# Expert loops of a mixture-of-experts layer, taken in steps of two pairs of tiles instead of one, with weights addressed in bytes

## The chip, the cores and the metric

The kernel runs on one NeuronCore of a Trainium2 chip. The metric is the device time of one launch in microseconds (us). PE is TensorE, DVE VectorE, ACT ScalarE, POOL GpSimd and SP SyncE, which computes nothing here and issues transfers. PEld is TensorE's loading of weights, which overlaps its products.

## The reference

The input is 128 sequences of 125 time steps with 64 channels. Three layers follow: a strided depthwise convolution with a norm over the whole sequence, a selective scan, and a mixture of experts. Only the last matters here; its core is, for 8064 tokens (128 x 63) of 64 channels:

```python
logits = xf @ Wr + br                                  # 64 experts
topk_logits, topk_idx = jax.lax.top_k(logits, 2)
gates = jax.nn.softmax(topk_logits, axis=1)
combine = zeros((T, E)).at[arange(T)[:, None], topk_idx].add(gates)
for e in range(E):
    h = relu(xf @ W1[e] + b1[e])                       # 64 -> 128
    y = h @ W2[e] + b2[e]                              # 128 -> 64
    out = out + combine[:, e:e + 1] * y
```

All of it is in float32.

## The kernel before

The kernel doesn't compute every expert for every token. It runs the experts' layers once for the tokens' first choice and once for their second (two halves). For each half it sorts the tokens by expert: VectorE works out a row number for every token, and GpSimd scatters the token rows to DRAM (`sorted_rows`), 63 indirect transfers of 128 rows each (line 438). Each expert's rows are padded to whole tiles of 128 rows, so a half has 126 tiles at most; two tiles are a pair, and a half has 63 pairs (`PAIRS`), 126 in all. The number of each tile's expert is worked out on the chip too and stands in `te`.

The expert stage goes over the 126 pairs. For each of them

- SyncE loads the packed weights of the two tiles' experts (first layer, second layer and bias beside each other, 193 floats per row, 128 rows) with two transfers (`load_weights`, line 328) into one of `WRING` = 7 slots, at an address read from a register. Before slot n % 7 is loaded again, SyncE waits until the outputs of pair n - 7 are copied out (`s_yb`). The expert numbers come into registers 32 at a time, once every 16 pairs (line 274). Token rows come for four pairs at once (`load_rows`, line 337), in a ring of four.
- TensorE transposes the pair's 128 x 128 block of token rows (`rows_T`, line 593), does the first-layer products of its two tiles, each on 64 rows of the array (`hidden`, line 600), and the output products (`outputs`, line 611), 192 columns wide, of which 64 are wanted.
- ScalarE copies the transposed block (`xT_copy`, line 812) and does bias and relu of the first tile (`relu_A`, line 819); VectorE does bias and relu of the second (`relu_B`, line 1162) and copies the outputs out (`y_copy`, line 1172). A float32 product shows as two matrix instructions in the trace, so a pair has one transpose, four first-layer and four output instructions.
- ScalarE's queue stores the outputs to DRAM (`store`, line 827, `expert_out`), from a ring of four (`YRING`).

The order on each engine is written out by hand: transposes run two pairs ahead of the outputs, first-layer products one pair ahead.

GpSimd's own order is: scatter of the first half, scatter of the second, gather of the first half's outputs (line 446) when its stores have landed, gather of the second half's. Each gather is again 63 indirect transfers. SyncE loads the first rows of the second half only when the second scatter has landed (`s_disp`). When gathered rows arrive, VectorE applies the gates and adds them up, and the result leaves.

Of the kernel before, what the change touches and what calls it, by code (L numbers as in the profile page):

```python
# [7 lines left out]
U32 = mybir.dt.uint32  # L8
ALU = mybir.AluOpType
# [4 lines left out]
P = 128  # L14
T_IN = 125
C = 64
# [31 lines left out]
WRING = 7  # L48
YRING = 4
WROW = HID + C + 1  # L50
OUT = 3 * C
CQ = -(-L // 8)
IDS = 32

# [21 lines left out]
def build(nc, x, w, b, gamma, beta, alpha, A_log, D_param, scale, W_dt, b_dt, W_B, b_B, W_C, b_C,  # L76
# [5 lines left out]
    with ExitStack() as ctx:  # L82
# [75 lines left out]
        xT_e = x_w1[:, o:o + 2 * P].rearrange("p (k n) -> p k n", k=2)  # L158
        o += 2 * P
        hT_e = x_w1[:, o:o + 4 * P].rearrange("p (k t n) -> p k t n", k=2, n=P)  # L160
        o += 4 * P
        y_e = x_w1[:, o:o + YRING * 2 * C].rearrange("p (k t d) -> p k t d", k=YRING, d=C)
# [109 lines left out]
        def experts(engine, g):  # L272

            return nc.values_load_multi_w_load_instructions(te[0:1, bass.ds(g, IDS)], engines=[engine],
                                                            min_val=0, max_val=E - 1, skip_runtime_bounds_check_because=
                                                            "te is a count of experts, clamped to E - 1")[1]
# [4 lines left out]
        def _(sp):  # L281
# [39 lines left out]

            def load_weights(h, q, es):

                n = h * PAIRS + q
                if n >= WRING:
                    sp.wait_ge(s_yb, n - WRING + 1)
                for t in range(2):
                    sp.dma_start(w_in[:, n % WRING, t, :], packed[bass.ds(es[t], 1), :, :].rearrange("a p n -> (a p) n")  # L328
                                 ).then_inc(s_win[n % WRING], 16)

            def load_rows(h, u):

                n = h * UNITS + u
                if n >= RING:
                    g, v = (n - RING) // UNITS, (n - RING) % UNITS
                    sp.wait_ge(s_rT, g * PAIRS + min(UNIT * (v + 1), PAIRS))
# [29 lines left out]
        def _(pool):  # L366
# [75 lines left out]
            for k, y in enumerate((y1, y2)):  # L442
                for j in range(YRING):
                    pool.wait_ge(s_st[j], 16 * (((k + 1) * PAIRS + YRING - 1 - j) // YRING))
# [7 lines left out]
        def _(pe):  # L452
# [135 lines left out]
            def rows_T(n):  # L588

                u = unit_of(n)  # L590
                if n % PAIRS % UNIT == 0:
                    pe.wait_ge(s_rows[u % RING], 16 * (u // RING + 1))
                pe.transpose(ps[:, n % 2, 0:P], rows_in[:, u % RING, n % PAIRS % UNIT, :], ident[:, :]).then_inc(s_rT, 1)  # L593

            def hidden(n):

                pe.wait_ge(s_win[n % WRING], 32 * (n // WRING + 1))
                pe.wait_ge(s_rTc, n + 1)
                for t in range(2):
                    last = pe.matmul(ps[:, 2 + 2 * (n % 2) + t, 0:P], w_in[t * C:(t + 1) * C, n % WRING, t, 0:HID],  # L600
                                     xT_e[t * C:(t + 1) * C, n % 2, :], start=True, stop=True)
                last.then_inc(s_hid, 1)

            def outputs(n):

# [4 lines left out]
                for t in range(2):  # L610
                    last = pe.matmul(ps[:, 6 + n % 2, t * OUT:(t + 1) * OUT], hT_e[:, n % 2, t, :],  # L611
                                     w_in[:, n % WRING, t, 0:OUT], start=True, stop=True)
# [14 lines left out]
            pe.wait_ge(s_yb, 2 * PAIRS)  # L627
# [24 lines left out]
        def _(act):  # L652
# [156 lines left out]
            def xT_copy(n):  # L809

                act.wait_ge(s_rT, n + 1)
                act.activation(xT_e[:, n % 2, :], ps[:, n % 2, 0:P], ACT.Copy).then_inc(s_rTc, 1)  # L812

            def relu_A(n):
# [425 lines left out]
```

## Time and profile before

| | |
|---|---|
| median of 3 runs | 884.67 us (881.72 to 885.47) |
| the profiled execution | 888.75 us |
| its span, first to last instruction | 886.8 us |
| PE, DVE, ACT, POOL busy | 501.2, 645.4, 339.2, 551.6 us |
| DMA traffic | 71.63 MB |
| mean granted clock of TensorE | 0.741 of full speed |

The profile comes from one execution, and its durations add up to its own time. Busy times are averages over stages with different limits: the convolution and the norms up to about 139 us, the scan up to about 446 us, routing and the first scatter up to about 612 us, the expert stage from 615 to about 797 us, the second gather and the sum up to the end. The expert stage is the one in which the change lies, and it is read from its own stretch.

### The profile page before, as it was taken

To read this page: it belongs to the slowest core of one execution; us is meant where nothing else is said; L and a number is where in the kernel's file an instruction comes from. 1 tells how busy PE (TensorE), PEld (TensorE's weight loads), DVE (VectorE), ACT (ScalarE), POOL (GpSimd) and SP (SyncE) were. 2 spreads that over 40 slices of the span, in tenths; PEclk is the share of its full clock that TensorE was granted. 3 is DMA by queue.
4 is the path that set the end of the run, shared out by engine and by line. 5 is a ranking of instruction groups with operands and counts; after the bars stand their busy time and mean duration, and the time that the engine had idled before them with its cause. 6 is when DMAs were issued, how large, how long until landed. Compare 5 with 4: busy or idle time off the path is not lost.

```text
span 886.8 us, 8725 instructions
## 1 busy us (share of the span) xinstructions
PE 501.2 (57%) x2132; PEld 320.0 (36%) x2132; DVE 645.4 (73%) x1160; ACT 339.2 (38%) x597; POOL 551.6 (62%) x398
## 2 busy tenths in 40 slices
PE   4916903365666665575556920002999999980340
PEld 3815801121211121121116910001777777760240
DVE  1379548999999989999974999991444444459951
ACT  2311384555555455454527710000444444430110
POOL 1002204699999999999940007777777167757774
PEclk9965655677787787878785555555999999995565
DMA  6999900000000000000000000302899899961131
GB/s 229 366 136 108 30 0 0 0 0 0 1 0 0 0 0 0 0 0 0 0 0 1 1 0 27 89 25 62 229 262 265 230 256 263 269 192 26 25 99 37
DMA packets 100734, 71.63 MB, mean 81 GB/s; under 512 B 29330, under 2 KB 87314, under 8 KB 100690
## 3 DMA queue, kind: packets, MB, share of 16 engines
q1 hardware_dynamic: 73154, 54.39, 28.0%
q0 software_dynamic: 8064, 8.27, 3.5%
q10 hardware_dynamic: 19472, 8.47, 3.3%
q8 instruction: 16, 0.26, 0.1%
q14 instruction: 28, 0.23, 0.1%
HBM read 48.12 MB, written 29.29 MB: 87 GB/s over the span
## 4 chain that ended last, share of the span: by engine, by line
POOL 35%; PE 22%; DVE 15%; issue 15%; SPq 4%; DMA 4%; ACT 3%; POOLq 1%; DVEq 0%; ACTq 0%
POOL hh_ring L419 13%; PE ps L611 8%; POOL w_ring L404 8%; POOL sorted_rows L438 7%; POOL xt L446 7%; PE ps L600 4%; DMA x_w<-packed 3%; PE ps L470 3%; SPq L328 2%; PE ps L538 2%; DVE mi L1072 1%; PE ps L521 1%; PE ps L593 1%; DVE hh_ring L1004 1%; DVE w_ring L1060 1%
## 5 line engine op out<-in xcount | busy, mean ns | idle before, releaser
L538 PE MATMUL ps<-hh_ring,ident 128*128 128x512 f32 x272 | 181.7, 807 | 153.1 <-POOL hh_ring L419 116.4
L438 POOL DMA_INDIRECT sorted_rows<-xp,slot_i x126 | 122.1, 969 | 115.0 <-DVE slot_i L1098 76.9
L404 POOL TENSOR_TENSOR w_ring<-xt,bc 128x1024 f32<-128x1024 f32 x64 | 153.8, 2405 | 37.3 <-DVE xt L973 37.3
L446 POOL DMA_INDIRECT xt<-expert_out,slot_i x126 | 120.7, 958 | 65.6 <-issue 37.8
L419 POOL TENSOR_TENSOR hh_ring<-hh_ring,bc 128x1024 f32<-128x1024 f32 x63 | 148.4, 2356 | 17.9 <-DVE hh_ring L1004 14.6
L538 PEld LDWEIGHTS ps<-hh_ring,ident 128*128 128x128 f32 x272 | 58.2, 234 | 275.8 <-POOL hh_ring L419 184.7
L1004 DVE TENSOR_TENSOR_SCAN hh_ring<-ps,w_ring 128x1024 f32<-128x1024 f32 x64 | 145.9, 2280 | 0.1
L611 PE MATMUL ps<-x_w 128*128 128x192 f32 x504 | 117.0, 355 | 0.0
L744 ACT ACTIVATE ps<-dt_t,a_exp 128x1024 f32<-128x1024 f32 x64 | 71.5, 1118 | 79.9 <-DVE w_ring L982 79.9
L748 ACT ACTIVATE ps<-dt_t,a_exp 128x1024 f32<-128x1024 f32 x64 | 71.5, 1118 | 65.1 <-DVE hh_ring L1004 65.1
L1172 DVE COPY x_w<-ps 128x128 f32<-128x128 f32 x126 | 36.8, 292 | 72.0 <-PE ps L611 69.0
L812 ACT ACTIVATE x_w<-ps 128x128 f32<-128x128 f32 x126 | 34.9, 278 | 135.1 <-PE ps L593 134.4
L611 PEld LDWEIGHTS ps<-x_w 128*128 128x128 f32 x504 | 79.7, 191 | 15.2 <-issue 0.4
L982 DVE TENSOR_TENSOR w_ring<-ps,w_ring 128x1024 f32<-128x1024 f32 x64 | 78.3, 1224 | 8.4 <-POOL w_ring L404 4.2
L998 DVE SCALAR_TENSOR_TENSOR w_ring<-ps,w_ring 128x1024 f32<-128x1024 f32 x64 | 76.8, 1200 | 0.0
L1162 DVE TENSOR_SCALAR x_w<-ps,x_w 128x128 f32<-128x128 f32 x126 | 44.3, 351 | 42.8 <-PE ps L600 40.4
L390 POOL TENSOR_TENSOR us_lg<-xp,vecs 128x1344 f32<-128x1344 f32 x3 | 9.2, 3069 | 88.5 <-DVE xp L926 88.5
L600 PE MATMUL ps<-x_w 64*128 64x128 f32 x504 | 62.9, 327 | 2.3 <-DMA x_w<-packed 1.8
L819 ACT ACTIVATE x_w<-ps,x_w 128x128 f32<-128x128 f32 x126 | 46.3, 368 | 24.1 <-PE ps L600 21.9
L600 PEld LDWEIGHTS ps<-x_w 64*128 64x128 f32 x504 | 38.7, 188 | 31.3 <-issue 25.3
L593 PE MATMUL ps<-ident,x_w 128*128 128x128 f32 x126 | 34.8, 278 | 16.7 <-DMA x_w<-sorted_rows 16.7
L584 PE MATMUL ps<-ident,tile_e 128*1 128x128 f32 x2 | 0.7, 373 | 55.6 <-DVE tile_e L1138 55.6
(174 smaller groups left out, 707.9 us busy)
## 6 DMA issues: line engine op xcount, KB each, us to landing
x_w<-packed SPq DMA_DIRECT2D x252, 96.5 KB
sorted_rows<-pad_rows SPq DMA_DIRECT2D x2, 4096.0 KB, 18.0
x_w<-sorted_rows SPq DMA_DIRECT2D x32, 256.0 KB
expert_out<-x_w ACTq DMA_DIRECT2D x126, 64.0 KB
packed<-in_L_ffn_W SPq DMA_DIRECT2D x3, 2048.0 KB, 36.2
x_w<-in_x SPq DMA_DIRECT2D x7, 448.0 KB, 10.1
sorted_rows<-xp,slot_i POOLq DMA_INDIRECT x126, 2.1
xt<-expert_out,slot_i POOLq DMA_INDIRECT x126, 2.4
```

The lines of the kernel that those rows point to most:

```text
L404: pool.tensor_tensor(w_ring[:, k % 4, :].rearrange("p (d s) -> p d s", s=S), up3[:, bass.ds(c * DC, DC), :], bc[:, k:k + 1, :].broadcast_t ...
L419: pool.tensor_tensor(hc_buf(k), h_buf(k), bc[:, N + k:N + k + 1, :].broadcast_to([P, DC, S]), ALU.mult).then_inc(s_hcp, 1)
L438: pool.indirect_dma_start(out=sorted_rows[k], out_offset=bass.IndirectOffsetOnAxis(ap=slot_i[:, k, l:l + 1], axis=0), in_=xp1[:, l, 0:C], ...
L446: pool.indirect_dma_start(out=y[:, l, :], out_offset=None, in_=expert_out[k], in_offset=bass.IndirectOffsetOnAxis(ap=slot_i[:, k, l:l + 1] ...
L538: ins = pe.matmul(ps[:, i, :], ident[:, :], hh_ring[:, buf, i * BANK:(i + 1) * BANK], start=(k < 0), stop=(k == N - 1), skip_group_check=True)
L600: last = pe.matmul(ps[:, 2 + 2 * (n % 2) + t, 0:P], w_in[t * C:(t + 1) * C, n % WRING, t, 0:HID], xT_e[t * C:(t + 1) * C, n % 2, :], start ...
L611: last = pe.matmul(ps[:, 6 + n % 2, t * OUT:(t + 1) * OUT], hT_e[:, n % 2, t, :], w_in[:, n % WRING, t, 0:OUT], start=True, stop=True)
L744: act.activation(banks(6, 2), d, ACT.Tanh, scale=a_exp[:, 2, k:k + 1]).then_inc(s_th, 1)
L748: act.activation(banks(2 + 2 * (k % 2), 2), d, ACT.Exp, scale=a_exp[:, 1, k:k + 1]).then_inc(s_dA, 1)
L982: dve.tensor_tensor(wv, banks(6, 2), wv, ALU.mult).then_inc(s_g, 1)
L998: dve.scalar_tensor_tensor(out=wv, in0=dA, scalar=1.0, in1=wv, op0=ALU.add, op1=ALU.mult).then_inc(s_b, 1)
L1004: dve.tensor_tensor_scan(hh_ring[:, k % 2, :], dA, wv, 0.0, ALU.mult, ALU.add).then_inc(s_h, 1)
```

## The change

Every loop of the expert stage goes in steps of two pairs (the 63rd pair of each half is a step of its own, so a half has 32 steps). In a step TensorE does two transposes into one PSUM bank, then eight first-layer instructions, then eight output instructions, which write both output banks (6 and 7) where one bank was used before. The semaphores count steps. ScalarE copies both transposed blocks with one instruction and does two bias-and-relu instructions; VectorE does two, and copies the outputs of both pairs with one; one store takes both. The weights' ring has eight slots instead of seven and is given back in steps: the weights of step i wait for the outputs of step i - 4. Slots of transposed rows, hidden rows and outputs are twice as large, as many as before.

`te` holds the expert's number times the bytes of an expert's block (98,816), multiplied on VectorE for all tiles at once. The weight transfers read the packed weights as bytes at that offset, where they read floats of block number e before.

```diff
-WRING = 7
+WRING = 8
 YRING = 4
+STEPS = -(-PAIRS // 2)
+BLOCK = 4 * P * WROW
+def pairs_of(i):
+    h, d = divmod(i, STEPS)
+    return range(h * PAIRS + 2 * d, h * PAIRS + min(2 * d + 2, PAIRS))
+def step_of(n):
+    return n // PAIRS * STEPS + n % PAIRS // 2
...
+            blocks = packed.rearrange("e p n -> (e p n)").bitcast(U8)
             def load_weights(h, q, es):
                 n = h * PAIRS + q
                 if n >= WRING:
-                    sp.wait_ge(s_yb, n - WRING + 1)
+                    sp.wait_ge(s_yb, step_of(n - WRING) + 1)
                 for t in range(2):
-                    sp.dma_start(w_in[:, n % WRING, t, :], packed[bass.ds(es[t], 1), :, :].rearrange("a p n -> (a p) n")
+                    sp.dma_start(w_in[:, n % WRING, t, :].bitcast(U8),
+                                 blocks[bass.ds(es[t], BLOCK)].rearrange("(p n) -> p n", p=P)
                                  ).then_inc(s_win[n % WRING], 16)
...
-            def hidden(n):
-                pe.wait_ge(s_win[n % WRING], 32 * (n // WRING + 1))
-                pe.wait_ge(s_rTc, n + 1)
-                for t in range(2):
-                    last = pe.matmul(ps[:, 2 + 2 * (n % 2) + t, 0:P], w_in[t * C:(t + 1) * C, n % WRING, t, 0:HID],
-                                     xT_e[t * C:(t + 1) * C, n % 2, :], start=True, stop=True)
+            def hidden(i):
+                for n in pairs_of(i):
+                    pe.wait_ge(s_win[n % WRING], 32 * (n // WRING + 1))
+                pe.wait_ge(s_rTc, i + 1)
+                for j, n in enumerate(pairs_of(i)):
+                    for t in range(2):
+                        last = pe.matmul(ps[:, 2 + 2 * (i % 2) + t, j * P:(j + 1) * P],
+                                         w_in[t * C:(t + 1) * C, n % WRING, t, 0:HID],
+                                         xT_e[t * C:(t + 1) * C, i % 2, j, :], start=True, stop=True)
                 last.then_inc(s_hid, 1)
-            def outputs(n):
-                pe.wait_ge(s_reluA, n + 1)
-                pe.wait_ge(s_reluB, n + 1)
-                if n >= 2:
-                    pe.wait_ge(s_yb, n - 1)
+            def outputs(i):
+                pe.wait_ge(s_reluA, i + 1)
+                pe.wait_ge(s_reluB, i + 1)
+                if i >= 1:
+                    pe.wait_ge(s_yb, i)
...
-            for n in range(2 * PAIRS):
-                if n + 2 < 2 * PAIRS:
-                    rows_T(n + 2)
-                if n + 1 < 2 * PAIRS:
-                    hidden(n + 1)
-                outputs(n)
+            for i in range(2 * STEPS):
+                if i + 2 < 2 * STEPS:
+                    rows_T(i + 2)
+                if i + 1 < 2 * STEPS:
+                    hidden(i + 1)
+                outputs(i)
...
-                dve.tensor_scalar(te[:, k * P:(k + 1) * P], ps[0:1, 2, 0:P], float(E - 1), None, ALU.min
+                dve.tensor_scalar(te[:, k * P:(k + 1) * P], ps[0:1, 2, 0:P], float(E - 1), float(BLOCK), ALU.min, ALU.mult
                                   ).then_inc(s_tei, 1)
```

On TensorE, in the middle of the expert stage, this stood before, for two pairs (`x_w1` holds the weights and the token rows, `ps` is PSUM; a matrix product here is one row):

```order
L593 MATMUL ps<-ident,x_w1 128x128
L600 MATMUL ps<-x_w1 128x128 [waits s_rTc,s_win4]
L600 MATMUL ps<-x_w1 128x128
L611 MATMUL ps<-x_w1 128x192 [waits s_yb,s_reluB,s_reluA]
L611 MATMUL ps<-x_w1 128x192
L593 MATMUL ps<-ident,x_w1 128x128
L600 MATMUL ps<-x_w1 128x128 [waits s_rTc,s_win5]
L600 MATMUL ps<-x_w1 128x128
L611 MATMUL ps<-x_w1 128x192 [waits s_yb,s_reluB,s_reluA]
```

And this stands on TensorE now, for one step:

```order
L610 MATMUL ps<-ident,x_w1 128x128 x2
L621 MATMUL ps<-x_w1 128x128 [waits s_rTc,s_win5,s_win4]
L621 MATMUL ps<-x_w1 128x128 x3
L634 MATMUL ps<-x_w1 128x192 [waits s_yb,s_reluB,s_reluA]
L634 MATMUL ps<-x_w1 128x192 x3
```

Each kind of product now stands in runs twice as long, and the first-layer run waits for the weights of both pairs at its start.

On SyncE, where the first loads wait for a slot, two pairs' weights stood before as (the ISA row multiplies the register):

```order
L328 ISA [waits s_yb]
L328 DMA x_w1<-packed 128x193
L328 ISA
L328 DMA x_w1<-packed 128x193
L328 ISA [waits s_yb]
L328 DMA x_w1<-packed 128x193
L328 ISA
L328 DMA x_w1<-packed 128x193
L337 DMA x_w1<-sorted_rows0 128x512
```

Now they stand on SyncE as:

```order
L343 DMA x_w1<-packed 128x772 [waits s_yb]
L343 DMA x_w1<-packed 128x772
L343 DMA x_w1<-packed 128x772 [waits s_yb]
L343 DMA x_w1<-packed 128x772
L353 DMA x_w1<-sorted_rows0 128x512 [waits s_rT]
```

The register instruction is gone; both waits of a step are for the same count, that of step i - 4, where each pair waited for its own before.

## Rows read from the trace of the kernel before

**Rows 1.** The page's head: span, and busy time of each engine.

```profile
span 886.8 us, 8725 instructions
PE 501.2 (57%) x2132; PEld 320.0 (36%) x2132; DVE 645.4 (73%) x1160; ACT 339.2 (38%) x597; POOL 551.6 (62%) x398
```

**Rows 2.** Windows: stretch, length, busy time (instructions) by engine, clock, DMA share, GB/s.

```profile
core 0: us, PE busy (x) PEld busy (x) DVE busy (x) ACT busy (x) POOL busy (x), PEclk, DMA share, GB/s
640.00:660.00 20.00, 19.71 (x131) 14.81 (x130) 9.16 (x29) 9.19 (x29) 15.13 (x17) 1.00 0.94 264
700.00:720.00 20.00, 19.47 (x127) 14.57 (x127) 9.02 (x29) 9.04 (x29) 6.05 (x7) 1.00 0.87 239
```

**Rows 3.** Timeline of one pair: start, length, engine, line, tiles, count, idle before.

```profile
652.64 0.27 PE L593 MATMUL ps<-ident,x_w 128*128 128x128 f32 x1
652.84 0.49 PE L600 MATMUL ps<-x_w 64*128 64x128 f32 x4
653.26 0.92 PE L611 MATMUL ps<-x_w 128*128 128x192 f32 x4
...
654.02 0.27 PE L593 MATMUL ps<-ident,x_w 128*128 128x128 f32 x1
...
654.29 0.29 DVE L1172 COPY x_w<-ps 128x128 f32<-128x128 f32 x1 [0.56 <-PE ps L611]
```

**Rows 4.** Timelines of TensorE over short stretches, same columns.

```profile
622.48 0.76 PE L611 MATMUL ps<-x_w 128*128 128x192 f32 x3
...
652.84 0.38 PE L600 MATMUL ps<-x_w 64*128 64x128 f32 x2
...
653.06 0.28 PE L600 MATMUL ps<-x_w 64*128 64x128 f32 x2
...
793.42 1.57 PE L611 MATMUL ps<-x_w 128*128 128x192 f32 x8
```

**Rows 5.** Waits in the expert stage: us in total, times, longest.

```profile
PEld ps L600 <- DMA x_w<-packed: 6.0, 15, 1.0
```

**Rows 6.** SyncE: instructions by line (ns minimum/median/maximum), a timeline row, its waits.

```profile
L328 SPq FUSED_REGOPS  x252: 37/37/51, 555.2 to 787.1; - x126
L328 SPq MOVE x_w<-packed x252: 29/29/38, 555.3 to 787.2; - x126
L328 SPq DMA_DIRECT2D x_w<-packed x252: 332/333/1693, 555.4 to 787.2; - x126
...
L337 SPq DMA_DIRECT2D x_w<-sorted_rows x32: 332/436/484, 612.1 to 780.6; - x32
...
L274 SPq TENSOR_LOAD <-te x8: 1916/2028/2227, 553.1 to 767.3; - x8
...
641.74 3.95 SPq L328 DMA_DIRECT2D x_w<-packed  x8
...
SPq L328 <- DVE x_w L1172: 11.1, 11, 6.4
```

**Rows 7.** The chain that ended last: start, length, what; transfers from issue to use.

```profile
612.07 2.77 DMA x_w<-sorted_rows
...
644.31 5.73 DMA x_w<-packed
...
727.27 3.23 DMA x_w<-packed
...
777.01 3.63 DMA x_w<-packed
```

**Rows 8.** Ends of scatters, turn of the halves, starts of gathers (chain and timelines).

```profile
609.91 2.14 DMA sorted_rows<-xp,slot_i
...
690.02 0.97 POOL L438 DMA_INDIRECT sorted_rows<-xp,slot_i  x1 [0.30 <-issue]
...
707.45 0.27 PE L593 MATMUL ps<-ident,x_w 128*128 128x128 f32 x1
708.75 0.33 ACTq L827 DMA_DIRECT2D expert_out<-x_w  x1
...
712.11 0.98 POOL L446 DMA_INDIRECT xt<-expert_out,slot_i  x1 [21.12 <-DMA expert_out<-x_w]
...
797.68 0.95 POOL L446 DMA_INDIRECT xt<-expert_out,slot_i  x1 [6.70 <-DMA expert_out<-x_w]
```

More of the change, by code:

```diff
@@ L8 @@
 U32 = mybir.dt.uint32
+U8 = mybir.dt.uint8
 ALU = mybir.AluOpType
@@ L274, in experts @@
             return nc.values_load_multi_w_load_instructions(te[0:1, bass.ds(g, IDS)], engines=[engine],
-                                                            min_val=0, max_val=E - 1, skip_runtime_bounds_check_because=
-                                                            "te is a count of experts, clamped to E - 1")[1]
+                                                            min_val=0, max_val=(E - 1) * BLOCK,
+                                                            skip_runtime_bounds_check_because="te is a count of experts, "
+                                                            "clamped to E - 1, times the bytes of a block")[1]
         block = ctx.enter_context(nc.Block())
@@ L443, in _ @@
                 for j in range(YRING):
-                    pool.wait_ge(s_st[j], 16 * (((k + 1) * PAIRS + YRING - 1 - j) // YRING))
+                    pool.wait_ge(s_st[j], 16 * (((k + 1) * STEPS + YRING - 1 - j) // YRING))
                 for l in range(L):
@@ L604, in outputs, with rows_T @@
-            def outputs(n):
-                pe.wait_ge(s_reluA, n + 1)
-                pe.wait_ge(s_reluB, n + 1)
-                if n >= 2:
-                    pe.wait_ge(s_yb, n - 1)
-                for t in range(2):
-                    last = pe.matmul(ps[:, 6 + n % 2, t * OUT:(t + 1) * OUT], hT_e[:, n % 2, t, :],
-                                     w_in[:, n % WRING, t, 0:OUT], start=True, stop=True)
+            def rows_T(i):
+                for j, n in enumerate(pairs_of(i)):
+                    u = unit_of(n)
+                    if n % PAIRS % UNIT == 0:
+                        pe.wait_ge(s_rows[u % RING], 16 * (u // RING + 1))
+                    last = pe.transpose(ps[:, i % 2, j * P:(j + 1) * P], rows_in[:, u % RING, n % PAIRS % UNIT, :],
+                                        ident[:, :])
+                last.then_inc(s_rT, 1)
@@ L613, in outputs @@
+            def outputs(i):
[3 more added lines that the diff above has]
+                    pe.wait_ge(s_yb, i)
+                for j, n in enumerate(pairs_of(i)):
+                    for t in range(2):
+                        last = pe.matmul(ps[:, 6 + j, t * OUT:(t + 1) * OUT], hT_e[:, i % 2, t, j, :],
+                                         w_in[:, n % WRING, t, 0:OUT], start=True, stop=True)
                 last.then_inc(s_yps, 1)
@@ L832, in _ @@
             relu_A(0)
-            for n in range(2 * PAIRS):
-                if n + 2 < 2 * PAIRS:
-                    xT_copy(n + 2)
-                if n + 1 < 2 * PAIRS:
-                    relu_A(n + 1)
-                if n > 0:
-                    store(n - 1)
-            store(2 * PAIRS - 1)
+            for i in range(2 * STEPS):
+                if i + 2 < 2 * STEPS:
+                    xT_copy(i + 2)
+                if i + 1 < 2 * STEPS:
+                    relu_A(i + 1)
+                if i > 0:
+                    store(i - 1)
+            store(2 * STEPS - 1)
             for q in range(CQ):
```

84 lines of the change are left out of this document (43 added, 41 removed).

## The prediction

> **What bounds the kernel now.** I read the page's head first: no engine is busy for more than 73% of the 886.8 us [rows 1], so stages have to be read one by one. The change touches the expert stage, from about 615 to 797 us. The windows of that stage show TensorE busy all the time at the full granted clock, and the DMA engines at 0.94 of their time while the scatter of the second half is still running, 0.87 without it [rows 2]. The timeline of one pair shows what TensorE's time consists of [rows 3]: transpose at 652.64, first-layer products from 652.84, output products from 653.26, next transpose at 654.02. The slots are 0.20, 0.42 and 0.76, together 1.38 us. From the third pair's outputs at 622.48 to the last but one's at 793.42 lie 122 pairs [rows 4], 1.401 us each, so only 0.02 per pair (2.3 us in all) is lost on waits. The waits agree: weights held TensorE's loads 15 times for 6.0 us in sum [rows 5].
>
> TensorE is thus the limit, but SyncE is close behind it. Eight weight loads are issued in 3.95 us, 0.52 each; every fourth pair a rows load (0.44), every sixteenth pair a load of expert numbers (2.03) [rows 6]. That is 1.04 + 0.11 + 0.13 = 1.28 us per pair of the 1.40 that there are. The chain of what ended last passes six times through a weight transfer, from its issue to the product that waited for it: 5.73 the first, 3.63 the last, 3.23 the shortest, 4.29 in the mean; with idle queues a transfer took 2.77 [rows 7].
>
> **What the change takes from TensorE.** Between two kinds of product the array does not go on at once. Inside a run of output products the starts are 0.163 apart (eight take 1.57, four 0.92 [rows 3, 4]), so a pair costs 0.65 inside a run and 0.76 as a run of its own. The first-layer products of the two tiles of a pair start together, in two groups 0.22 apart [rows 4], so a second pair adds 0.22 to a run of 0.42. A transpose has 128 columns against 192, so inside a run about 0.163 x 128/192 = 0.11 against 0.20. A step of two pairs takes 0.31 + 0.64 + 1.41 = 2.36 us, 1.18 per pair. Unhindered, 124 pairs would save (1.401 - 1.18) x 124 = 27 us. Bounds: 0 if every pair kept its whole slot.
>
> **What it does to SyncE.** The register multiplication before each weight load goes: 37 ns [rows 6] and a gap of about 39 ns (eight loads in 3.95 us are (3950 - 333)/7 = 517 ns apart, less 333, 37 and 29, over three gaps), so a load costs 0.44 instead of 0.52. Byte type itself I cost at nothing: the transfer still moves rows of 772 B. A step then needs 4 x 0.44 + 0.44/2 + 2.03/8 = 2.23 us, just under TensorE's 2.36.
>
> **What it does to the ring, the term that decides.** A slot is free when the copy of its outputs is done. Before, pair n waits for the copy of pair n - 7; from there to the products of n lie five whole pairs and a transpose minus the copy, 5 x 1.38 + 0.20 - 0.56 = 6.5 us, of which issue and landing use about 4.7. Now step i waits for the copy of step i - 4; from there to its products lie only two whole steps and a transpose: 2 x 2.36 + 0.31 - 0.69 = 4.3 us (copy end 0.56 after the run [rows 3], plus 0.13 for 128 more columns; 0.56 and 0.85 are the bounds). And it must issue four loads first. So the ring of four steps closes on itself. Once round: first-layer run 0.64, outputs of the step before 1.41, transposes 0.31, next first-layer run 0.64, own outputs 1.41, copy 0.69, together 5.10. Then SyncE: three loads ahead of the last 1.32, half a rows load 0.22, an eighth of the expert numbers 0.25, together 1.79. Then the landing L of the last load. Four steps, eight pairs: (6.89 + L)/8 us per pair.
>
> L is bounded by 2.77 and 5.73. The six in the chain are ones that somebody waited for, so their mean of 4.29 is somewhat high for before; but without spare time the later of four loads counts, not of two. I take the mean of the six and the idle one, (6 x 4.29 + 2.77)/7 = 4.07. That gives 1.370 per pair against 1.401, and 124 x 0.031 = 3.8 us. TensorE's 27 us are nearly all spent waiting for weights.
>
> **What else moves.** VectorE and ScalarE do the same biases and relus in two instructions per step; their copies have twice the columns; both have idle time to spare in this stage. Outputs of a step now use both PSUM banks, so they wait for the copy of the step before: that ends 0.69 after its run, the next run starts 0.31 + 0.64 = 0.95 after it, so 0.26 us is left over. Without that cover it would cost up to 64 x 0.4 us. Stores have 1024 B rows instead of 512: fewer packets, which I leave in L. The last store of the first half is issued after the first-layer run and the relus of a whole step: 0.31 + 0.64 + 0.12 + 0.74 = 1.8 after the outputs end, against 1.3 before (707.45 to 708.75), 0.5 us later [rows 8]. GpSimd's gathers follow: it waited 21 us for that store and 6.70 for the second half [rows 8], so both halves' gains count. Sum: 3.8 - 0.5 = 3.3 us; with hops of semaphores, which I have no row for, I say 2.7. The profiled execution took 888.75 us (1.95 beyond its span) and would take 886.0; against the median, 884.67 - 2.7 = 882.0.
>
> **The rivals.** (a) *The landing is short and the ring keeps up*, L below about 3.4. Then (6.89 + 3.4)/8 = 1.29 or less, and other limits take over. The second scatter's last issue is at 690.02 and lands 2.14 later [rows 8]; SyncE then issues one rows load, the expert numbers and four weight loads (0.44 + 2.03 + 1.32), the last lands 3.4 later at 699.4, and the first half's outputs end 0.64 + 0.76 later at 700.8, 6.6 us before 707.45, 6.1 with the later store. In the second half GpSimd can gain only its 6.70 of waiting. The cap is 12.8 us: 872. For it: the long landings of the chain are the selected ones. Against it: DMA share 0.94. The Trainium skill's "DMA: Bandwidth & Descriptors" (the anatomy of one DMA) would have this case: a fixed 2.0 us plus bytes at 436 GB/s, an estimate of 2.2 us for 98.8 KB; it is a fit for the software queue, and the idle 2.77 here is already above it. Chance 0.27.
>
> (b) *Slower: the landing grows.* If L is 4.8, between the six's mean and their longest, a pair takes 1.461 and the kernel gets 7.4 + 0.5 us slower: 892.6. It decides at L = 4.3, where the ring gives the 1.401 of before; in bursts of four, each load queues behind three. For it: 4.83, 4.94 and 5.73 in the chain. Against it: SyncE rests between bursts, and 2.77 is what a rested queue shows. The same page (latency and other measured facts) says that HBM latency goes from 0.2 us to 2 under high load; the 2.77 against 5.73 [rows 7] fit such a growth. Chance 0.26.
>
> (c) *TensorE saves nothing by pairing*: then the run of first-layer products is 0.84, which lengthens the ring by 0.4 us per turn, 0.05 per pair: 888. The starts of [rows 4] speak against it. Chance 0.05.
>
> The forecast, a ring that gives back most of what TensorE saves (L from 3.8 to 4.3: 877 to 886), has 0.42. A measurement of this kernel tells 0.5%, 4.4 us, from no change. Faster by more than that: (a) and a third of the forecast, 0.41. Within: 0.35. Slower: 0.24. The range takes the cap on one side and L = 4.8 on the other: 872 to 892.
>
> **What would show it.** In the trace after: within a step the starts 0.31, 0.64 and 1.41 apart where nothing is late; a stall of several tenths before the first-layer run of most steps, ended by weights, some 20 us in sum (before 6.0); SyncE waiting for the output copy for 25 us or more (before 11.1 [rows 6]); its loads 0.44 apart with no register instruction; GpSimd's first gather at about 709 instead of 712.1. The prediction is wrong if those waits are small (a), if steps take over 2.8 us (b), or if byte-wise loads show other packets or longer issues.

## The result and the profile after

On the chip of the first timing the changed kernel took 889.75 us (median of 20 runs, 885.94 to 896.83) and the kernel before, beside it, 886.24 us (20 runs). The ratio is 1.0048, 95% interval 1.0032 to 1.0065: 4.3 us slower (2.8 to 5.8), where 2.7 us faster was forecast. The profiled execution took 896.83 us, 7 us above its own median, so its losses are larger than usual; that of the kernel before took 888.75, 2.5 above its median.

The head of its page, and three windows of the expert stage, which answer to [rows 1] and [rows 2]:

```profile
span 894.8 us, 8039 instructions
PE 481.8 (54%) x2132; PEld 323.3 (36%) x2132; DVE 630.0 (70%) x1098; ACT 321.7 (36%) x535; POOL 551.5 (62%) x398
```

```profile
640.00:660.00 20.00, 18.00 (x137) 15.50 (x134) 7.85 (x23) 7.68 (x23) 15.19 (x16) 1.00 0.94 268
...
700.00:720.00 20.00, 16.25 (x109) 13.55 (x108) 6.43 (x19) 6.41 (x19) 4.67 (x5) 0.91 0.76 208
...
687.50:691.00 3.50, 3.50 (x18) 2.85 (x17) 1.03 (x3) 1.01 (x3) 1.73 (x2) 0.52 0.73 195
```

TensorE has 19 us less to do, VectorE 15, and the whole is longer. TensorE is no longer busy all the time, and its clock, at 1.00 all through this stage before, falls to half in places (third window). The timeline of TensorE over a step and the start of the next, beside [rows 3]:

```profile
652.02 0.38 PE L610 MATMUL ps<-ident,x_w 128*128 128x128 f32 x2
652.33 0.71 PE L621 MATMUL ps<-x_w 64*128 64x128 f32 x8
652.98 1.57 PE L634 MATMUL ps<-x_w 128*128 128x192 f32 x8
654.39 0.38 PE L610 MATMUL ps<-ident,x_w 128*128 128x128 f32 x2
655.30 0.72 PE L621 MATMUL ps<-x_w 64*128 64x128 f32 x8 [0.54 <-issue]
```

The starts are 0.31, 0.65 and 1.41 apart, as forecast. But the next first-layer run comes 0.91 after its transposes instead of 0.31: its weights were late. Over the expert stage (610 to 815 us) the waits of TensorE and then those of SyncE read:

```profile
PEld ps L621 <- issue: 34.1, 58, 2.9
PE ps L621 <- issue: 22.9, 27, 2.7
...
PEld ps L621 <- DMA x_w<-packed: 5.4, 6, 1.2
```

```profile
SPq L343 <- DVE x_w L1200: 36.0, 30, 8.5
```

Most stalls are put down to "issue": the profile names no single releaser there. The trace's semaphore records do. In the two stretches that are compared below, 29 of 47 first-layer runs start 0.09 us after the last of their weights has landed; before, it was 9 of 92 pairs. I call such a run **late**. Of the 34.1 us a part is the natural gap in front of each run (0.17 in an undisturbed step, some 10 in all); some 25 to 30 us, with the last row, were lost on weights, against 6.0 before [rows 5]. SyncE waited 36.0 us for the output copy, against 11.1 [rows 6]. GpSimd's gathers, which answer to [rows 8], started later: the first by 2.0 us, the second by 8.1.

```profile
714.12 0.98 POOL L462 DMA_INDIRECT xt<-expert_out,slot_i  x1 [24.57 <-DMA expert_out<-x_w]
...
805.77 0.98 POOL L462 DMA_INDIRECT xt<-expert_out,slot_i  x1 [12.78 <-DMA expert_out<-x_w]
```

**One turn of the ring.** The timeline shows what a late step waited for (PE, DVE and SPq rows of one stretch):

```profile
639.55 0.71 PE L621 MATMUL ps<-x_w 64*128 64x128 f32 x8 [0.17 <-issue]
...
640.20 1.57 PE L634 MATMUL ps<-x_w 128*128 128x192 f32 x8
...
641.88 0.42 DVE L1200 COPY x_w<-ps 128x256 f32<-128x256 f32 x1 [0.96 <-PE ps L634]
...
642.01 0.72 PE L621 MATMUL ps<-x_w 64*128 64x128 f32 x8
...
642.33 1.83 SPq L343 DMA_DIRECT2D x_w<-packed  x4
...
644.40 0.72 PE L621 MATMUL ps<-x_w 64*128 64x128 f32 x8
...
647.46 0.72 PE L621 MATMUL ps<-x_w 64*128 64x128 f32 x8 [0.62 <-issue]
```

The first-layer run at 639.55 is followed by the output run at 640.20, the copy that frees four slots (ends 642.30), the four loads into them (642.33, the last issued at 643.74), and the first-layer run that needed them at 647.46. In between stand two other first-layer runs (642.01 and 644.40). So a turn takes 7.91 us and covers **three** steps, not four. From the first-layer start to the end of the copy it is 2.75 us (0.64 + 1.41 + 0.69 = 2.74 forecast), SyncE's three loads ahead of the last 1.41, the rest 3.72, from the issue of the last load to the products.

The same can be read from the records for every late run of the stage, 35 of the 57 from the seventh step to the last but one. The mean turn over three steps takes 8.65 us: 2.86 to the end of the copy, 0.69 until SyncE begins with the four loads, 1.48 to the issue of the last, 3.54 until it has landed, 0.09 to the products. SyncE doesn't always begin when the copy ends: 0.03 us after it where nothing is in the way, but 1.1 to 2.9 us after it for the loads of steps 8, 16, 24, 32, 40, 48 and 56 (counted from 0) and for some behind them. Right ahead of each of these stands a load of expert numbers, about 2 us each (the first of the eight rows counted here lies ahead of the stage):

```profile
L286 SPq TENSOR_LOAD <-te x8: 1881/1992/2254, 551.7 to 773.7; - x8
```

SyncE's instructions by line (ns minimum, median, maximum), beside [rows 6]:

```profile
L343 SPq MOVE x_w<-packed x252: 29/29/38, 553.8 to 794.9; - x126
L343 SPq DMA_DIRECT2D x_w<-packed x252: 332/381/2486, 553.8 to 795.0; - x126
```

The register multiplication is gone, but an issue takes 381 ns in the median instead of 333. Four loads take 1.83 us, (1.83 - 0.42)/3 = 0.47 apart, where 0.44 was forecast and 0.52 stood before.

### The profile page after: what moved, and what is told of

Same layout as the page of the kernel before. It is cut to its first block, busy times and chain, and to the rows that moved or that the text cites. A ratio compares the mean times of both kernels' runs of the same rounds, so it can differ in the third digit from the quotient of the medians.

```text
span 894.8 us, 8039 instructions
## 1 busy us (share of the span) xinstructions
PE 481.8 (54%) x2132; PEld 323.3 (36%) x2132; DVE 630.0 (70%) x1098; ACT 321.7 (36%) x535; POOL 551.5 (62%) x398
## 4 chain that ended last, share of the span: by engine, by line
POOL 34%; PE 23%; issue 17%; DVE 16%; ACT 3%; SPq 3%; DMA 3%; POOLq 1%; DVEq 0%; ACTq 0%
POOL hh_ring L435 13%; PE ps L634 9%; POOL w_ring L420 8%; POOL sorted_rows L454 7%; POOL xt L462 7%; PE ps L621 4%; PE ps L486 3%; PE ps L554 2%; PE ps L537 2%; DMA x_w<-packed 2%; DVE mi L1099 1%; PE ps L610 1%; SPq L343 1%; DVE hh_ring L1031 1%; DVE w_ring L1087 1%
## 5 line engine op out<-in xcount | busy, mean ns | idle before, releaser
L554 PE MATMUL ps<-hh_ring,ident 128*128 128x512 f32 x272 | 178.3, 793 | 155.1 <-POOL hh_ring L435 118.0
L634 PE MATMUL ps<-x_w 128*128 128x192 f32 x504 | 104.0, 350 | 1.1 <-DVE x_w L1200 1.1
L1190 DVE TENSOR_SCALAR x_w<-ps,x_w 128x128 f32<-128x128 f32 x126 | 38.5, 347 | 73.0 <-PE ps L621 72.4
L634 PEld LDWEIGHTS ps<-x_w 128*128 128x128 f32 x504 | 84.7, 198 | 9.7 <-issue 3.0
L1200 DVE COPY x_w<-ps 128x256 f32<-128x256 f32 x64 | 26.9, 421 | 66.7 <-PE ps L634 66.7
L836 ACT ACTIVATE x_w<-ps 128x256 f32<-128x256 f32 x64 | 24.3, 380 | 134.2 <-PE ps L610 132.0
L621 PE MATMUL ps<-x_w 64*128 64x128 f32 x504 | 48.3, 310 | 26.5 <-issue 22.9
L845 ACT ACTIVATE x_w<-ps,x_w 128x128 f32<-128x128 f32 x126 | 39.4, 363 | 50.2 <-PE ps L621 49.6
L621 PEld LDWEIGHTS ps<-x_w 64*128 64x128 f32 x504 | 36.6, 198 | 39.5 <-issue 34.1
L610 PE MATMUL ps<-ident,x_w 128*128 128x128 f32 x126 | 25.4, 285 | 16.6 <-DMA x_w<-sorted_rows 16.2
```

The source lines that it names most:

```text
L554: ins = pe.matmul(ps[:, i, :], ident[:, :], hh_ring[:, buf, i * BANK:(i + 1) * BANK], start=(k < 0), stop=(k == N - 1), skip_group_check=True)
L621: last = pe.matmul(ps[:, 2 + 2 * (i % 2) + t, j * P:(j + 1) * P], w_in[t * C:(t + 1) * C, n % WRING, t, 0:HID], xT_e[t * C:(t + 1) * C, i ...
L634: last = pe.matmul(ps[:, 6 + j, t * OUT:(t + 1) * OUT], hT_e[:, i % 2, t, j, :], w_in[:, n % WRING, t, 0:OUT], start=True, stop=True)
```

## The experiments

These ran on three other chips: all x and z runs on one, the w runs but the last on a second, w4 on a third. The kernel before takes 1076 to 1083 us on all three (medians 1081.5 and 1080.3, 1082.9, 1075.8), and I call them the slow chips. Each ratio is against the kernel before on the same chip in the same batch, so ratios, and rates read from traces, are compared here, not times with those above; w1 against an x or z run is also a comparison between two chips. Where the 195 us more are spent shows in two windows of the changed kernel's trace there (w1), one beside GpSimd's second scatter and one after it:

```profile
640.00:690.00 50.00, 4.55 (x18) 3.83 (x18) 1.22 (x4) 1.64 (x5) 33.88 (x35) 0.50 0.07 24
695.00:795.00 100.00, 80.77 (x568) 69.07 (x567) 33.55 (x98) 33.09 (x99) 0.00 (x0) 0.92 0.75 208
```

While GpSimd issues its indirect transfers there, the expert loops nearly stand still. Only when it rests do they run. The same holds for its first gather (800 to 870 us). The **quiet stretches**, in which GpSimd moves nothing, are therefore the place to read the ring. I give the mean time per pair in them: from the ninth first-layer run to the 37th (28 steps, 55 pairs), and from the 43rd to the 62nd (19 steps, 38 pairs); for kernels with steps of one pair, from the 15th run to the 71st and from the 87th to the 123rd. The first stretch reaches 2 to 8 us into the first gather; z3's is cut at its 65th run, because 15 us of it would lie there. The last column counts the late runs in both stretches, as far as the records are complete. Each rate comes from one execution.

| kernel | ratio, 95% interval | us per pair, quiet stretches | late runs |
|---|---|---|---|
| x3, one pair, byte addresses | 1.0009 (0.9985 to 1.0033) | 1.380, 1.380 | 0 of 91 |
| w2, one pair, ring of 10, early release | 0.9983 (0.9959 to 1.0008) | 1.380, 1.380 | 0 of 92 |
| z3, one pair, ring of 5 | 1.0254 (1.0189 to 1.0318) | 1.590, 1.561 | 32 of 86 |
| w1, the changed kernel | 0.9957 (0.9932 to 0.9982) | 1.441, 1.360 | 24 of 46 |
| x1, changed, float addresses | 1.0028 (1.0001 to 1.0054) | 1.433, 1.426 | 26 of 46 |
| z2, changed, half the bytes | 0.9954 (0.9923 to 0.9985) | 1.373, 1.307 | 22 of 47 |
| x4, changed, early release | 0.9931 (0.9904 to 0.9958) | 1.358, 1.325 | 23 of 46 |
| z4, changed, release per pair | 0.9905 (0.9870 to 0.9940) | 1.406, 1.306 | 22 of 46 |
| x2, changed, ring of 10 | 0.9908 (0.9876 to 0.9939) | 1.356, 1.328 | 6 of 47 |
| z1, ring of 10 and early release | 0.9872 (0.9827 to 0.9917) | 1.322, 1.243 | 0 of 46 |
| w3, the same kernel again | 0.9879 (0.9832 to 0.9927) | 1.306, 1.228 | 1 of 46 |
| w4, changed, ring of 6 | 1.0414 (1.0384 to 1.0444) | 1.824, 1.795 | 27 of 45 |

On the first chip the same stretches of the changed kernel, with GpSimd at work beside them, gave 1.484 and 1.486 per pair, and those of the kernel before 1.417 and 1.393.

**x1, float addresses.** The changed kernel, weights read as floats at a block number again, so the multiplication before each load is back.

```diff
-                    sp.dma_start(w_in[:, n % WRING, t, :].bitcast(U8),
-                                 blocks[bass.ds(es[t], BLOCK)].rearrange("(p n) -> p n", p=P)
+                    sp.dma_start(w_in[:, n % WRING, t, :], packed[bass.ds(es[t], 1), :, :].rearrange("a p n -> (a p) n")
```

> The changed kernel with its weights read as floats at a block number again (one register multiplication before each load). Theory ring (a step's weights are let go too late, the ring of four steps closes on itself): loads 0.52 apart instead of 0.475, three of them ahead of the last, so 3 x 0.04/8 = 0.016 us per pair, 2 us more than the changed kernel: 1.007 of the kernel before. Theory bytes (byte-wise loads are what costs: their issue took 0.38 instead of 0.33): the issue is back at 0.33 and the kernel is at or under 1.000. If the 0.38 comes from issues that follow each other closely, it is back at 0.33 with no gain.

Measured: 1.0028, a little below the 1.007 that the ring gave. The issue is back at 333 ns in the median (381 in the changed kernel) without a gain:

```profile
L343 SPq DMA_DIRECT2D x_w<-packed x252: 3/333/1987, 550.9 to 947.6; - x126
```

In the changed kernel, too, issues that came after a pause took 333. So the longer issue comes from following closely, and the bytes are no cost. Whether they gain anything in the two-pair ring stays open: the changed kernel had 0.9957, but on another chip, and its first quiet stretch is no faster (1.441 against 1.433).

**x2, a ring of ten pairs.**

```diff
-WRING = 8
-YRING = 4
+WRING = 10
+YRING = 3
```

> The changed kernel with ten slots of weights (five steps) instead of eight, the room taken from the output ring (three steps instead of four). Theory ring: the round now takes five steps, (6.89 + 4.1)/10 = 1.10 us per pair, so other limits take over: TensorE's 1.18, SyncE's about 1.2; the stage gets some 13 us shorter until GpSimd's chain caps it; 0.985 to 0.99 of the kernel before. Theory traffic (the DMA engines can't bring weights faster than some 265 GB/s): the landing grows with the deeper ring and the time stays within 0.3% of the changed kernel, 1.002 to 1.008.

Measured: 0.9908, at the edge of what the ring gave and far from what traffic gave. Only 6 of 47 runs are late, against 24 of 46 in the changed kernel (w1): the ring was what held it.

**x3, bytes alone.** The kernel before with byte offsets, steps of one pair and its own ring of seven.

```diff
-                    sp.dma_start(w_in[:, n % WRING, t, :], packed[bass.ds(es[t], 1), :, :].rearrange("a p n -> (a p) n")
+                    sp.dma_start(w_in[:, n % WRING, t, :].bitcast(U8),
+                                 blocks[bass.ds(es[t], BLOCK)].rearrange("(p n) -> p n", p=P)
```

> The kernel before with the byte part of the change alone. Theory ring: SyncE is not the limit there, so 1.000 within 0.2%; its loads 0.475 apart, its recovery after a load of expert numbers a little quicker. Theory bytes: byte-wise loads land later or issue more slowly, 1.003 or more.

Measured: 1.0009, no difference. TensorE sets the pace, 1.38 us per pair without exception in the quiet stretches (starts of two first-layer runs in its timeline):

```profile
740.93 0.49 PE L605 MATMUL ps<-x_w 64*128 64x128 f32 x4
...
742.32 0.49 PE L605 MATMUL ps<-x_w 64*128 64x128 f32 x4
```

**x4, early release.** SyncE waits for the output products of step i - 4, the last that read the weights, instead of for the copy of what they wrote.

```diff
-                    sp.wait_ge(s_yb, step_of(n - WRING) + 1)
+                    sp.wait_ge(s_yps, step_of(n - WRING) + 1)
```

> The changed kernel, with SyncE waiting for the output products of step i - 4 and not for the copy behind them (the weights' last reader is the product). Theory ring: 0.69 us leave the round, 0.69/8 = 0.086 us per pair, up to 10 us of the stage, less what fewer falls of the clock add: 0.990 to 0.995 of the kernel before. Theory traffic: within 0.3% of the changed kernel.

Measured: 0.9931. It takes the copy's 0.69 us out of the turn and changes nothing else. The interval overlaps that of w1 on the other chip, so the time alone doesn't tell the two apart. In the quiet stretches a pair takes 0.06 us less than in the changed kernel (1.345 against 1.408 over both). A turn over three steps would give 0.69/6 = 0.115; the sign fits, the size is half. About half of the runs were late, and steps without a stall can't get shorter.

**z1, both.** The edits of x2 and x4 together.

```diff
+WRING = 10
+YRING = 3
...
+                    sp.wait_ge(s_yps, step_of(n - WRING) + 1)
```

> The changed kernel with both cures of the ring: ten slots of weights (output ring of three steps), and SyncE waiting for the output products instead of their copy. Theory ring: the round is (6.89 - 0.69 + 4.1)/10 = 1.03 us per pair, far under TensorE's 1.18 and SyncE's 1.2, so it adds little to the ten slots alone (0.9908 of the kernel before): 0.985 to 0.990, near the cap by GpSimd's chain. Theory traffic: no better than either cure alone, 0.991 to 0.995.

Measured: 0.9872, the best of all, as the ring gave. No run is late any more.

**z2, half the bytes.** The changed kernel with only the first 388 of each row's 772 bytes loaded; it leaves out the last 31 of the first layer's 128 columns, the whole second layer and the bias (more than the expectation says).

```diff
-                    sp.dma_start(w_in[:, n % WRING, t, :].bitcast(U8),
-                                 blocks[bass.ds(es[t], BLOCK)].rearrange("(p n) -> p n", p=P)
+                    sp.dma_start(w_in[:, n % WRING, t, 0:97].bitcast(U8),
+                                 blocks[bass.ds(es[t], BLOCK)].rearrange("(p n) -> p n", p=P)[:, 0:388]
```

> The changed kernel with weight transfers of 388 B per row instead of 772 (the second half of each row, with the bias and most of the second layer, is left out, so the outputs are not the reference's); as many transfers, instructions and waits. Theory ring: only the landing gets shorter, by the transfer's own share of it, some 0.3 us, so 0.3/8 = 0.04 us per pair, up to 5 us: 0.998 to 1.001. Theory traffic: weights were 60% of the stage's bytes; with half of them the stage runs at TensorE's 2.36 per step, the cap of 12 us is reached, 0.987 to 0.992.

Measured: 0.9954, between the two ranges and in neither. It is the same as the changed kernel (w1, 0.9957) within the intervals, though its quiet stretches are 0.06 per pair faster. From the issue of a step's last load to its landing the median there is 2.52 us, against 3.23 in w1. So half the bytes take 0.7 us off the landing, more than the 0.3 expected; most of it stays.

**z3, one pair, a ring of five.** The kernel before with `WRING = 5`, which gives steps of one pair a ring about as tight as the changed kernel's.

```diff
-WRING = 7
+WRING = 5
```

> The kernel before with five slots of weights instead of seven, still one pair at a time. Theory ring: once round five pairs are 0.42 + 0.76 + 0.20 + 0.42 + 0.76 + 0.56 = 3.1 us, one load of 0.52 ahead, 0.24 for rows and expert numbers, and a landing of 3.4 to 4.1: 7.3 to 8.0 over 5, so 1.45 to 1.6 us per pair instead of 1.40; 6 to 25 us more, 1.007 to 1.028. Theory traffic: fewer slots don't change a rate set by the DMA engines, 1.000 to 1.003.

Measured: 1.0254 (three executions), as the ring gave. A tight ring slows steps of one pair as well. TensorE's loads now wait for weights; from 725 to 785 us:

```profile
PEld ps L600 <- DMA x_w<-packed: 11.8, 26, 1.3
```

**z4, release per pair.** Output products count pairs, and SyncE waits for those of pair n - 8.

```diff
-                    sp.wait_ge(s_yb, step_of(n - WRING) + 1)
+                    sp.wait_ge(s_yps, n - WRING + 1)
...
-                last.then_inc(s_yps, 1)
+                    last.then_inc(s_yps, 1)
...
-dve.wait_ge(s_yps, i + 1)
-act.wait_ge(s_yps, i - 1)
+dve.wait_ge(s_yps, pairs_of(i)[-1] + 1)
+act.wait_ge(s_yps, pairs_of(i - 2)[-1] + 1)
```

> The changed kernel, with TensorE counting the output products pair by pair and SyncE waiting for the pair n - 8 itself. Theory ring: the first pair's loads of a step start 0.65 + 0.69 us earlier than in the changed kernel, the second's 0.69, and SyncE's own 1.8 us of issue are partly hidden: better than waiting for the step's products (0.9931), 0.985 to 0.992. Theory traffic: as that one, 0.993.

Measured: 0.9905, within the range, but not to be told from x4. A reason can be argued, not shown: the second pair's slots come free no earlier than in x4, and it is the second pair's weights that a step waits for last.

**w1, the changed kernel on a slow chip.** No edit.

> The changed kernel, unaltered, beside the kernel before on the same chip as the variants. Theory 1 (a ring that closes on itself passes every disturbance on): a ratio above 1, some 1.002 to 1.008, and clearly above every variant whose ring was loosened (0.987 to 0.993 so far). Rival (the loosened variants were faster only because that chip treats the kernel before badly, where it hops often between engines): then the changed kernel is faster there too, 0.990 to 0.995, and the variants prove little about the ring.

Measured: 0.9957 (0.9932 to 0.9982), slightly faster than before, where I expected slower. The first half of the rival is thereby met: on the slow chips the changed kernel loses nothing. Yet it is slower per pair in the first quiet stretch (1.441 against 1.380 in x3) and hardly faster in the second (1.360). What it gains may lie in the stretches that crawl: from first to last first-layer run it takes 311.0 us, x3 317.7. But this trace is of its fastest execution, 6.7 us under its median, so that isn't shown. The second half of the rival, that the variants prove little about the ring, falls on w3, on this same chip: 0.9879 (0.9832 to 0.9927), 0.8% beyond w1, clear of its interval, with 1 late run for 24. For x2, x4 and z4 alone the times are only 0.3 to 0.5% beyond w1 and on another chip.

**w2, a loose ring with steps of one pair.** The kernel before with `WRING = 10`, `YRING = 3` and the early release.

```diff
-WRING = 7
-YRING = 4
+WRING = 10
+YRING = 3
...
-                    sp.wait_ge(s_yb, n - WRING + 1)
+                    sp.wait_ge(s_yps, n - WRING + 1)
```

> Steps of one pair as before, with a ring of ten pairs and slots given back by the output products instead of by the copy. If the loosened ring alone gave the variants their gain, this gains as much as they do, 0.987 to 0.990. If the gain needs both (steps of two pairs save TensorE's time, the ring lets it be used), this one saves at most the 2.3 us that pairs of before lose on waits: 0.997 to 1.001. The second is what theory 1 says, since before has only 6.0 us of weight waits to lose.

Measured: 0.9983 (0.9959 to 1.0008), as theory 1 says. A loose ring alone brings next to nothing. The gain needs both: two-pair steps, and a ring that lets TensorE use them.

**w3, the best again.** The kernel of z1.

> The best variant again (ring of ten pairs, slots given back by the output products, steps of two pairs). Theory 1: 0.984 to 0.992 whichever chip it is, 8 to 14 us below the changed kernel, since rows of the scatter still bound where the first half can begin and the gathers bound the tail. Rival (a gain of the one chip's crawling stretches only): within 0.5% of before on a chip without them.

Measured: 0.9879, on the chip of w1; in its trace most steps take 2.36 or 2.37 us. TensorE's and SyncE's waits from 725 to 785 us:

```profile
PEld ps L610 <- DMA x_w<-sorted_rows: 4.9, 4, 1.7
PEld ps L621 <- issue: 4.0, 23, 0.2
```

```profile
SPq L343 <- PE ps L634: 4.0, 8, 1.5
SPq L353 <- PE ps L610: 0.2, 1, 0.2
```

Weights are no longer waited for (0.17 per step is the natural gap); now and then the token rows are. SyncE rests 4.2 of 60 us, so it is probably the next limit; no run takes work from it alone.

**w4, a ring of six.** The changed kernel with `WRING = 6`, to tell apart two ways of counting the turn.

```diff
-WRING = 8
+WRING = 6
```

> The changed kernel with six weight slots instead of eight: step i waits for the copy of step i - 3. It tells apart two ways to count the ring. As the prediction counted it (a turn is one TensorE step of 2.36, then first-layer run, outputs, copy, SyncE and landing, 6.89 + L, over as many steps as there are slots), a step takes (6.89 + 4.07)/3 = 3.65 us. As a ring that closes from the first-layer run of the next step (0.64, outputs 1.41, copy 0.69, SyncE 1.79, landing L: 4.53 + L, over one step fewer than there are slots), a step takes (4.53 + 4.07)/2 = 4.30 us. In the stretches of the expert stage in which GpSimd moves nothing the starts of first-layer runs should therefore lie 3.5 to 3.8 apart by the first count and 4.1 to 4.6 by the second; with eight slots they lie 2.80 apart there in the mean. About 50 of the 64 steps lie in such stretches, so the ratio to the kernel before is about 1.035 by the first and 1.06 to 1.07 by the second.

Measured: 1.0414, between the two ratios expected, and 3.58 and 3.59 us per step in the quiet stretches (one of the first 28 steps holds a single pair), in the range of the first count. The structure says otherwise. In TensorE's timeline short and long steps alternate:

```profile
732.17 0.72 PE L621 MATMUL ps<-x_w 64*128 64x128 f32 x8 [2.04 <-issue]
...
734.54 0.72 PE L621 MATMUL ps<-x_w 64*128 64x128 f32 x8
...
739.99 0.72 PE L621 MATMUL ps<-x_w 64*128 64x128 f32 x8 [3.02 <-DMA x_w<-packed]
...
742.36 0.72 PE L621 MATMUL ps<-x_w 64*128 64x128 f32 x8
```

The steps are 2.37, 5.45, 2.37: one is late, the next is not, the one after it is again. That is a turn of two steps in a ring of three. And the landings that stand in its chain are far shorter than the 4.07 that both counts had put in (all eight of 725 to 795 us):

```profile
728.54 2.16 DMA x_w<-packed
...
735.37 3.84 DMA x_w<-packed
...
750.21 2.20 DMA x_w<-packed
...
756.75 2.27 DMA x_w<-packed
...
763.41 3.49 DMA x_w<-packed
...
780.08 2.60 DMA x_w<-packed
...
787.03 2.29 DMA x_w<-packed
...
793.78 2.55 DMA x_w<-packed
```

Their mean is 2.68. With it the first count gives (6.89 + 2.68)/3 = 3.19 us per step, the second (4.53 + 2.68)/2 = 3.60. Measured: 3.58 and 3.59. So the second holds, with a landing that I took from this trace; my expectation was off because it took the landing as fixed. The late runs of this trace agree: their turns over two steps take 7.2 us in the mean, with 2.6 for the landing.

## Why the prediction was wrong

**Right.** TensorE's slots (0.31, 0.64, 1.41) came out to the hundredth, and so did the output copy inside the turn. That the ring closes on itself, that TensorE's 27 us go into waits for weights (about 20 forecast, 25 to 30 measured), and that SyncE waits for the copy for 25 us or more (36.0) was right too. x2, x4, z1 and z3 each changed the ring alone (x2 and z1 with one output slot less) and moved time and late runs in the way that says so, and w3 against w1 shows it on one chip; w2 shows that the ring of before had room.

**The step that failed: the turn.** The prediction went once round as "first-layer run .64, outputs of the step before 1.41, transposes .31, next first-layer run .64, own outputs 1.41, copy .69" and divided by four steps. But the first 2.36 of these are one whole TensorE step that has no stall in it, and the stalls are what the term was to find. The products of step i wait for the copy of step i - 4, and the outputs of step i - 4 run right behind the first-layer run of step i - **3**. So the shortest loop goes from the first-layer start of step i - 3 to that of step i: 0.64 + 1.41 + 0.69, SyncE's 1.79, the landing L, over three steps. That is (4.53 + L)/6 per pair. With the prediction's own L of 4.07 it gives 1.433, where (6.89 + L)/8 gave 1.370. Over 124 pairs, 1.433 is 4.0 us more than the 1.401 of before, and the forecast would have been slower by some 4.5 us with the later store. Slower by 4.3 was measured. A loop that contains a step without a stall understates the loops that contain none. The bound between gain and loss was thereby L = 3.88, not 4.3, and the forecast's L stood on the other side of it.

That 4.5 comes so near to 4.3 is partly luck, as two terms were off by about as much in opposite ways (see below). With the landing as measured, 3.54, the prediction's own formula gives (6.89 + 3.54)/8 = 1.304, some 12 us faster: it misses by more, not less, once its input is right.

What speaks for the three steps is the turn at 639.55, w4's alternating steps, and w4's rate. The same count for steps of one pair with a ring of five (four pairs per turn: 0.42 + 0.76 + 0.56, SyncE 0.52 + 0.24, L) gives (2.50 + 4.07)/4 = 1.64; z3 measured 1.590 and 1.561, and its late turns took 6.48 us over four pairs, 1.62 each, with 3.16 for the landing.

**Terms that were off.** The landing was put at 4.07. In the changed kernel it is 3.54 in the mean for late runs (3.40 over all steps), and the four transfers in its chain in the expert stage, 4.18, 4.16, 1.99 and 3.62, have a mean of 3.49. It hadn't grown: in the same two stretches of the trace before it is 3.41 in the mean, so the six of the chain with their 4.29 were a selection of long ones. Nor was 2.77 the idle landing of a weight load: the row at 612.07 [rows 7] is a load of token rows, 256 KB and not 98.8, and the shortest weight loads take about 2.0. The landing isn't a constant either. In w4, whose loads come in separate bursts, it was 2.68, and half the bytes took 0.7 off it.

SyncE's part was put at 1.79 and is 0.69 + 1.48 = 2.17. The load of expert numbers was spread over eight steps as 0.25 each, but it comes at once, and the steps behind it are late by it. And a weight load, put at 0.44, measured 0.47, because an issue that follows closely on another takes 0.38 and not 0.333. The rows load of 0.436 in [rows 6] had this sign already. A step then needs 4 x 0.47 + 0.22 + 0.25 = 2.35 us of SyncE, no longer "just under TensorE's 2.36" but the same: once late, SyncE hardly catches up. No run took the number loads out, so what they cost by themselves is open.

The Trainium skill's "DMA: Bandwidth & Descriptors" (anatomy of one DMA) has a transfer as a fixed 2.0 us plus bytes at 436 GB/s, an estimate of 2.2 for such a load and 2.1 for half of one; the fit is for transfers issued by GpSimd. The shortest landings here, 1.99 and 2.16, are near it. The others, 3.54 in the mean while the DMA engines were busy for 0.76 to 0.94 of the time, are not, and z2's 0.7 is more than the 0.1 between these estimates.

**Not foreseen: the clock.** After stalls of about 2 us and more TensorE ran at half clock in four places, the lower of its two levels (1.2 instead of 2.4 GHz), for 3.4 us each. The timeline shows it:

```profile
685.97 0.71 PE L621 MATMUL ps<-x_w 64*128 64x128 f32 x8 [1.95 <-issue]
...
688.40 0.63 PE L610 MATMUL ps<-ident,x_w 128*128 128x128 f32 x2
688.96 1.23 PE L621 MATMUL ps<-x_w 64*128 64x128 f32 x8
690.12 2.00 PE L634 MATMUL ps<-x_w 128*128 128x192 f32 x8
691.96 0.38 PE L610 MATMUL ps<-ident,x_w 128*128 128x128 f32 x2
```

In the step at 688.40 the runs take 0.56, 1.16 and 1.84 instead of 0.31, 0.64 and 1.41, so 1.2 us more. The four places are at 687.6, 711.5, 732.0 and 755.9, each 7 to 13 us behind a load of expert numbers (675.2, 698.8, 723.3, 748.5). At 1.2 us each that is an estimate of some 5 us in all; that the profiled execution was 7 us above its median may be this, which I didn't test. The Trainium skill's "TensorE: Matmul & The Clock Gate" (what's actually happening) says that an idle array falls back to the lower level; the trace agrees in the two levels, though this array was idle for only 2 to 2.8 us between two runs. Before, with stalls of 0.7 us at most in the middle of the stage, the granted clock stayed at 1.00. Not every stall of this length does it: the w4 rows above show stalls of 2 and 3 us, with the slots of the full clock behind them.

**The rivals.** (b) named the right side and the right place, but took a landing of 4.8 for it; the landing didn't grow. (a) had the landing nearly right (3.4 at most, against 3.4 to 3.5) and still failed: with such a landing the ring doesn't keep up. (c) failed: the slots are as forecast. The byte addresses cost nothing, as said, although the longer issues that were named as a sign against it did come; x3 and x1 show it.

**Open.** The ratio differs by chip, 1.0048 on the first and 0.9957 on a slow one, and with it the sign. Why is not shown. None of the variants was measured on the first chip; there the ring is shown by the trace alone (29 late runs of 47), and its part in the 4.3 us isn't told apart from that of SyncE's late starts and of the clock.

## What to carry to other kernels

A ring of slots that is given back late is a loop. Write down which run each link follows. Of the loops that you find take the one that spans the fewest steps and has no whole step of the bounding engine inside it, and divide by the steps that this loop spans, not by the number of slots. Take the landing from all transfers of the stage, not from those in the chain that ended last, and keep a rare long instruction on the issuing engine as the burst that it is. Doubling a step doubles what is given back at once, so with nearly the same memory the ring loses slack. On the first chip eight slots in steps of two gave less than seven in steps of one; on a slow chip ten slots with an earlier release turned a gain of 0.4% into one of 1.2%. Where such a loop is near the engine's own pace, a stall can cost twice, as in the four places where the clock fell behind it.

## What the runs showed of the hardware

On the slow chips the program took about 195 us longer. The nearest trace to the kernel before there is x3's: its first first-layer run starts at 640.0 us (615.9 on the first chip), its last 317.7 us later (177.1), and its span ends 123.4 us after that (93.8). So 141 of the 195 us lie in the expert loops, where they run beside GpSimd's indirect transfers. Engines wait there for up to 26.8 us at a time, for a releaser that the profile can't name (waits of the changed kernel from 800 to 870 us):

```profile
DVE x_w L1190 <- remote: 37.0, 2, 26.8
ACT x_w L845 <- remote: 30.1, 2, 21.3
```

On the first chip the loops run beside scatter and gather at 1.4 to 1.5 us per pair. I have no cause for this.

A weight load's issue on SyncE takes 333 ns after a pause, and also 0.18 us behind another with the register multiplication between them (before and x1, 0.515 apart). It takes 381 ns when it follows by less than 0.1 us (the changed kernel, x3), so that loads come 0.474 apart in the median, 0.425 at the least. With the multiplication gone the pause between two issues shrank from 182 to 93 ns and the issue grew by 48.
